# Four graph layers on one core: the message bias copied into PSUM by ScalarE, and 1/rms spread over the partitions by two DMAs

## What is computed

```python
# layer 0
agg = eps * x + adj @ x
h = silu(rmsnorm(agg @ W1 + b1) * rms_weight)      # 512 hidden columns
x = layernorm(x + h @ W2 + b2)
# layer 1
x_conv = relu(bn(conv17(relu(bn(conv1(x))))) + x)
s = x @ w_se.T + b_se
A = exp(-squared_distances(s))
msg = relu(x @ w_msg.T + b_msg)
x = layernorm(x + gru([x_conv, A @ msg], x))
# layer 2: three hops with adj / row_sum(adj), weighted sum, leaky relu
# layer 3
x = layernorm(x + relu(((1 + eps) * x + adj @ x) @ W1 + b1) @ W2 + b2)
```

## Time and profile before

| what | us |
|---|---|
| median of 3 runs (lowest, highest) | 1133.11 (1129.41, 1134.9) |
| the profiled execution's own time | 1131.74 |
| its span in the trace | 1129.9 |

### The profile page before, as it was taken

How to read it: one execution, slowest core, us unless ns; L and a number is a source line. 1 busy time by engine, 2 the same in 40 slices (tenths; PEclk the granted TensorE clock), 3 DMA queues, 4 the chain that set the end, 5 groups by cost and what they waited for, 6 DMA issues and landing times.

```text
span 1129.9 us, 24862 instructions
## 1 busy us (share of the span) xinstructions
PE 1074.6 (95%) x8043; PEld 961.1 (85%) x8043; DVE 818.6 (72%) x2549; ACT 709.2 (63%) x1305; POOL 613.6 (54%) x652
## 2 busy tenths in 40 slices
PE   7899999999999959989999999999999999999875
PEld 6799999999999959967888888888888888888764
DVE  4477787777778733624788787878787878788984
ACT  4445555555555532345677787877777777777765
POOL 1244433434343306634466777777777777777865
PEclk9999999999999989989999999999999999999999
DMA  4112323222322126841211121212121212100001
GB/s 162 57 48 84 94 94 95 84 90 90 95 94 85 57 82 205 249 153 48 60 45 57 48 67 48 66 48 67 48 66 48 67 48 67 48 20 19 20 29 38
DMA packets 64190, 84.45 MB, mean 75 GB/s; under 512 B 6464, under 2 KB 33472, under 8 KB 63808
## 3 DMA queue, kind: packets, MB, share of 16 engines
q1 hardware_dynamic: 64064, 82.86, 23.2%
HBM read 57.14 MB, written 25.69 MB: 73 GB/s over the span
## 4 chain that ended last, share of the span: by engine, by line
PE 89%; DVE 4%; issue 3%; POOL 2%; ACT 1%; DMA 1%; SPq 0%; ACTq 0%; DVEq 0%; POOLq 0%
PE banks L160 18%; PE banks L154 12%; PE banks L155 10%; PE banks L156 10%; PE banks L515 10%; PE banks L774 4%; PE banks L684 3%; PE banks L543 3%; PE banks L608 3%; PE banks L659 2%; PE banks L485 2%; PE banks L637 2%; PE banks L575 1%; PE banks L611 1%; PE banks L613 1%
## 5 line engine op out<-in xcount | busy, mean ns | idle before, releaser
L167 POOL TENSOR_TENSOR rstd<-ve,minus_half 128x4 f32<-128x4 f32 x128 | 131.1, 1025 | 52.5 <-DVE ve L1088 49.1
L167 POOL TENSOR_TENSOR r_rms<-ms,minus_half 128x4 f32<-128x4 f32 x32 | 32.3, 1009 | 223.9 <-DVE ms L1052 223.9
L515 PE MATMUL banks<-w,s 128*128 128x128 f32 x768 | 101.2, 275 | 0.4 <-DVE y L1066 0.4
L515 PEld LDWEIGHTS banks<-w,s 128*128 128x128 f32 x768 | 95.6, 192 | 3.3 <-issue 0.5
L154 PE MATMUL banks<-agg_hi,w_hi 128*128 128x512 f32 x192 | 84.3, 439 | 3.2 <-ACT agg_hi L164 3.0
L1078 DVE BATCH_NORM_STATS2 stats<-y 128x6 f32<-128x128 f32 x384 | 82.6, 276 | 2.2 <-POOL y L1445 2.0
L156 PE MATMUL banks<-agg_hi,w_lo 128*128 128x512 f32 x192 | 76.1, 396 | 0.0
L155 PE MATMUL banks<-agg_lo,w_hi 128*128 128x512 f32 x192 | 76.1, 396 | 0.0
L1420 POOL TENSOR_TENSOR y<-ya,yb 128x512 f32<-128x512 f32 x32 | 41.6, 1299 | 63.2 <-PE banks L724 62.5
L1406 POOL TENSOR_TENSOR x_lo<-x1c,x_hi 128x512 fp32r<-128x512 f32 x32 | 41.2, 1287 | 62.7 <-ACT x_hi L164 62.7
L160 PE MATMUL banks<-at,x_rows 128*128 128x128 f32 x512 | 69.7, 280 | 3.9 <-DVE agg_lo L1040 3.0
(11 more groups left out here) (197 smaller groups left out, 3369.8 us busy)
## 6 DMA issues: line engine op xcount, KB each, us to landing
at<-in_at SPq DMA_DIRECT2D x32, 256.0 KB, 2.9
x_rows<-in_x SPq DMA_DIRECT2D x32, 256.0 KB, 2.9
x_scratch<-x SPq DMA_DIRECT2D x32, 256.0 KB, 3.2
ad<-in_ad SPq DMA_DIRECT2D x32, 256.0 KB, 2.6
x1c<-x_scratch SPq DMA_DIRECT2D x32, 256.0 KB, 2.6
atc<-in_at SPq DMA_DIRECT2D x32, 256.0 KB, 3.0
yh<-yh_scratch SPq DMA_DIRECT2D x64, 128.0 KB, 3.4
out<-out_rows SPq DMA_DIRECT2D x32, 256.0 KB, 2.0
```

What stands on the lines that cost most here:

```text
L167: return nc.gpsimd.tensor_tensor(to[:], base[:], minus_half[:], ALU.pow)
L515: last = pe.matmul(bank[7][:, g, :], s[c][:, g, :], w2[:, c, :], start=(c == 0 and g == 0), stop=(c == H0 - 1), skip_group_check=True)
```

## The change

1. PE's and ACT's `spread_rms` go. SP stores r_rms (128 x 4, one value of 4 bytes each) to DRAM as 4 x 128, waits for it, and loads these 2 KB into each of 128 partitions of rv, which becomes a ring of two. `rms` on POOL waits for the store of the group before.
2. `messages` has no bias product. ACT's `message_bias` copies the bias row, repeated for the four graphs, into bank 4, and the products add to it. One product at the start of the third stage marks the bank as written.
3. All engines' orders in the first and third stage are new, and the banks are dealt out anew, with the waits of `free` that belong to them. Depths in turns change: `hidden` 2 and 3, `down`, `residual0`, `apply0`, `row_sums` come a turn later in the first stage, `gram` in the turn of its group; agg_hi and agg_lo are double. x_rows has five tiles, ad has one.
4. The start flag in `by_graph` stands on the first of four products. The three startup tiles share memory with hn. POOL's `minus_mean` counts on r2's and r3's semaphores. The preparation of `msg_bias` and `pick` (two memsets, two copies on ACT, one subtraction on DVE) goes.

Tiles and constants:

```diff
-        X_RING, AT_RING, AD_RING, X1_RING = 4, 2, 2, 2
+        X_RING, AT_RING, AD_RING, X1_RING, RV_RING = 5, 2, 1, 2, 2
...
             for g in range(G):
-                last = pe.matmul(psum[:, g, :], lhs(g), rhs(g), start=True, stop=True)
+                last = pe.matmul(psum[:, g, :], lhs(g), rhs(g), start=(g == 0), stop=(g == G - 1),
+                                 skip_group_check=True)
...
+        agg = rows("agg")
+        agg_hi, agg_lo = ([rows(f"agg_{n}{i}", F32R) for i in range(2)] for n in ("hi", "lo"))
+        rv = [rows(f"rv{i}") for i in range(RV_RING)]
...
-        TURNS1 = GROUPS + 11
+        TURNS1 = GROUPS + 12
```

SP:

```diff
             def load_ad(k):
                 until(sp, "row_sum", k - AD_RING)
                 sp.dma_start(ad[k % AD_RING][:], w["ad"][k]).then_inc(ad_in[k % AD_RING], 16)
+            def store_rms(k):
+                until(sp, "r_rms", k)
+                landed(sp, rv_in, k - 2)
+                sp.dma_start(rms_dram[k].rearrange("g n -> n g"), r_rms[:],
+                             allow_slow_non_contiguous=True).then_inc(rms_stored[k % 2], 16)
+            def load_rv(k):
+                landed(sp, rms_stored, k)
+                until(sp, "hn2", k - RV_RING)
+                sp.dma_start(rv[k % RV_RING][:], rms_dram[k].unsqueeze(0).to_broadcast([P, G, P])
+                             ).then_inc(rv_in[k % RV_RING], 16)
...
                 stage(load_at, t + 2)
                 if t >= 2:
                     stage(load_x, t + 1)
+                stage(store_rms, t - 1)
+                stage(load_rv, t - 1)
+                stage(load_ad, t + 1 - 12)
                 stage(store_x1, t - 6)
-                stage(load_ad, t + 2 - 11)
```

PE, first stage:

```diff
-            def spread_rms(k):
-                until(pe, "r_rms", k)
-                free(pe, ("hcp", k - 7), ("rv", k - 1))
-                for g in range(G):
-                    last = pe.transpose(bank[4][:, g, :], r_rms[:, g:g + 1].to_broadcast([P, P]), ident[:])
-                last.then_inc(sem["spread"], 1)
...
             def conv1(k):
                 until(pe, "x1", k)
-                free(pe, ("rv", k + 6), ("hcp", k - 1))
-                by_graph(pe, bank[4], lambda g: x1[k % X1_RING][:, g, :], lambda g: conv1_w[:]
+                free(pe, ("ms", k + 7), ("prod", k + 7), ("hcp", k - 1))
+                by_graph(pe, bank[5], lambda g: x1[k % X1_RING][:, g, :], lambda g: conv1_w[:]
...
                 if half == 0:
-                    free(pe, ("hn3", k + 8), ("xh0", k - 1))
+                    free(pe, ("hn0", k + 8), ("xh0", k - 1))
                 else:
-                    free(pe, ("hn2", k + 8), ("ms", k + 8), ("xh1", k - 1))
-                psum = flat(bank[(3, 1)[half]])
+                    free(pe, ("hn1", k + 8), ("xh1", k - 1))
...
             for t in range(TURNS1):
                 stage(neighbours, t)
+                stage(down, t - 4, 3)
+                stage(hidden, t - 2, 3)
+                stage(square_sums, t - 1)
+                stage(hidden, t - 2, 2)
                 stage(conv1, t - 8)
+                stage(transform, t - 10, 1)
+                stage(down, t - 3, 0)
+                stage(hidden, t - 1, 1)
+                stage(transform, t - 10, 0)
+                stage(down, t - 3, 1)
+                stage(x1_t, t - 5)
+                stage(hidden, t - 1, 0)
                 stage(down, t - 3, 2)
-                stage(gram, t - 1)
-                stage(x1_t, t - 5)
-                stage(down, t - 3, 3)
-                stage(transform, t - 10, 0)
-                stage(transform, t - 10, 1)
-                stage(hidden, t - 1, 0)
-                stage(hidden, t - 1, 3)
-                stage(square_sums, t - 1)
-                stage(hidden, t - 1, 1)
-                stage(hidden, t - 1, 2)
-                stage(down, t - 2, 0)
-                stage(spread_rms, t - 1)
-                stage(down, t - 2, 1)
+                stage(gram, t)
```

PE, third stage (of the order only the lines of the new one):

```diff
             def messages(k):
                 landed(pe, x1c_in, k)
-                free(pe, ("z0", k - 8), ("c2_res", k), ("v", k - 2), ("msg", k - 1))
-                pe.matmul(flat(bank[7]), pick[:], flat(msg_bias), start=True, stop=False, skip_group_check=True)
+                until(pe, "msg_set", k)
                 for g in range(G):
-                    last = pe.matmul(bank[7][:, g, :], x1c[k % X1C_RING][:, g, :], msg_w[:], start=False,
+                    last = pe.matmul(bank[4][:, g, :], x1c[k % X1C_RING][:, g, :], msg_w[:], start=False,
                                      stop=(g == G - 1), skip_group_check=True)
                 last.then_inc(sem["msg_ps"], 1)
...
+            landed(pe, x1c_in, 0)
+            pe.matmul(flat(bank[4]), ident[:], flat(x1c[0]), start=True, stop=True).then_inc(set_pe, 1)
...
                 stage(codes, t)
+                stage(inverse, t - 1)
+                stage(hidden3, t - 9, 1)
+                stage(gate_x, t - 2, R_GATE)
+                stage(messages, t - 1)
                 stage(down3, t - 9, 0)
+                stage(distances, t)
                 stage(y1_t, t - 5)
                 stage(down3, t - 9, 1)
+                stage(gate_nmp, t - 2, R_GATE)
+                stage(hop2, t - 6)
+                stage(hidden_n, t - 2)
+                stage(gate_conv, t - 2, R_GATE)
+                stage(gather3, t - 8)
+                stage(prop_in, t - 5)
+                stage(hop3, t - 6)
                 stage(gate_nmp, t - 2, N_GATE)
                 stage(gate_x, t - 2, Z_GATE)
                 stage(gate_conv, t - 2, N_GATE)
                 stage(gate_nmp, t - 2, Z_GATE)
+                stage(hop1, t - 5)
                 stage(gather, t - 1)
+                stage(hidden3, t - 8, 0)
                 stage(gate_conv, t - 2, Z_GATE)
```

ACT (of the orders only the new ones):

```diff
-            def spread_rms(k):
-                until(act, "spread", k)
-                until(act, "hn2", k - 1)
-                copy(rv[:], bank[4][:]).then_inc(sem["rv"], 1)
...
+                stage(silu, t - 3, 2)
+                stage(silu, t - 3, 3)
                 stage(full, t)
                 stage(high, t)
+                stage(x1_full, t - 6)
+                stage(spectrum_of, t - 10, 1)
+                stage(conv1, t - 9)
+                stage(spectrum_of, t - 10, 0)
+                stage(silu, t - 2, 1)
+                stage(silu, t - 2, 0)
...
+            def message_bias(k):
+                free(act, ("ghn", k - 2), ("msg", k - 1))
+                if k == 0:
+                    act.wait_ge(set_pe, PE_PROP + 1)
+                copy(bank[4][:], msg_row.unsqueeze(1).to_broadcast([P, G, P])).then_inc(sem["msg_set"], 1)
...
+                stage(factors, t, 0)
                 stage(factors, t, 1)
+                stage(hidden3, t - 9, 0)
+                stage(conv_high, t - 2)
+                stage(gate_z, t - 3)
+                stage(x1_high, t - 1)
                 stage(hidden3, t - 9, 1)
                 stage(message, t - 1)
+                stage(apply3, t - 10)
+                stage(edges, t)
+                stage(hidden_n, t - 2)
                 stage(gate_r, t - 2)
+                stage(agg3, t - 8)
+                stage(message_bias, t)
+                stage(apply2, t - 7)
                 stage(gate_n, t - 3)
+                stage(multiple, t - 5, 3)
+                stage(leaky_relu, t - 6)
                 stage(conv_full, t - 1)
+                stage(multiple, t - 5, 2)
+                stage(multiple, t - 5, 1)
+                stage(multiple, t - 5, 0)
                 stage(nmp_high, t - 1)
```

DVE, first stage:

```diff
-                until(dve, "rv", k)
+                landed(dve, rv_in, k)
                 until(dve, ("s0", "s1", "s2", "s3")[c], k - 1)
-                V.scalar_tensor_tensor(out=hn[c][:], in0=bank[(5, 0, 1, 3)[c]][:], scalar=column("b1", c), in1=rv[:],
+                V.scalar_tensor_tensor(out=hn[c][:], in0=bank[(3, 0, 2, 6)[c]][:], scalar=column("b1", c),
+                                       in1=rv[k % RV_RING][:],
                                        op0=ALU.add, op1=ALU.mult).then_inc(sem[("hn0", "hn1", "hn2", "hn3")[c]], 1)
...
             for t in range(TURNS1):
+                stage(apply0, t - 5)
                 stage(product, t - 1)
-                stage(apply0, t - 4)
-                stage(residual0, t - 3)
+                stage(normalise, t - 3, 2)
+                stage(residual0, t - 4)
                 stage(mean_square, t - 1)
-                stage(stats0, t - 3)
+                stage(normalise, t - 2, 1)
+                stage(stats0, t - 4)
+                stage(low, t)
+                stage(normalise, t - 2, 0)
+                stage(moments, t - 4, 0, LN_EPS)
+                stage(normalise, t - 2, 3)
+                stage(row_sums, t - 12)
                 stage(conv1_bias, t - 8)
-                stage(low, t)
-                stage(moments, t - 3, 0, LN_EPS)
-                stage(row_sums, t - 11)
-                stage(normalise, t - 1, 1)
```

(35 more changed lines are left out.)

235 lines of the change are left out of this document (94 added, 141 removed).

## The result

The changed kernel takes **1214.26 us** (median of four, 1211.53 to 1215.42) against 1132.44 us of the kernel before: ratio 1.0719, 95% interval 1.0694 to 1.0744. The forecast was 1115 (1101 to 1128). The profiled execution took 1214.68 us, its span is 1212.9 us.

A forecast was written before the change was run, and what follows sets the result against it. PE, busy 95% of the span, was taken to bound the full turns of the first and third stages. Terms -14.1 - 7.4 + 5 - 3 + 1 + 1 + 0.3 = -17.2 us took 1131.7 to 1114.5, called 1115 (1101 to 1128).

The forecast's parts named there:

- Transposes off PE: First stage: four transposes per group leave PE, 0.44 us each group in the chain, 32 x 0.44 = -14.1 us.
- Round trip: First stage: storing r_rms and loading rv takes 4 + 2.9 us, bounds 4.8 to 10.8, hidden behind other work: 0 us.
- Fill: Start of the first stage: normalise waits some 3 us, but PE's early turns are shorter: 0 (-2 to +3).
- Order and drain: First stage's drain: apply0 heads DVE's turn, so three turns get shorter, less some slow start: -3 us (-6 to 0).
- tight copies: First stage, full turns: spectrum copies out of banks 0 and 3 must be over in 1.3 us: +1 (0 to 3).
- Ring of ad: Start of second stage: one ad tile delays row sums and POOL's sixth negation, so PE waits: +5 us (0 to +8).
- Bias: Third stage: one 128x512 bias product per group leaves PE, 0.23 us in the chain, 32 x 0.23 = -7.4 us.
- Sum: Whole kernel: all terms together make -17.2 us, taking the profiled 1131.7 us to 1114.5.
- Rival A: First stage: 1/rms returns late, normalise waits each turn, low and gram behind it; slower, 1154 us at 13 us; chance 0.10.
- Rival B: First or third stage: tight handovers slip 0.3 to 0.5 us per turn, some 12 us: 1127 us; chance 0.14.
- C: Start of second stage: the single ad tile costs nothing: 1110 us, or 1105 with a faster drain; chance 0.12.
- D: First and third stages: waits replace each removed piece, PE's turns stay 11.56 and 18.94 us: 1133 us; chance 0.02.

The follow-up runs named there:

- apart: Changed kernel with the 4-byte pieces of r_rms stored 64 bytes apart and rv loaded from one fixed 2 KB row: 1115.08 us, ratio 0.9843.
- pe_spread2: Changed kernel with 1/rms spread again by four transposes on TensorE, ScalarE's copy of rv placed ahead of its relu: 1129.72 us, ratio 0.9973.
- bias_pe: store16 plus ScalarE reordering rv, the last five turns' ad loaded into freed x_rows tiles, and the message bias back on TensorE: 1124.68 us, ratio 0.9935.
- delay2: store16 with rv loaded three times, each load waited for before the next: 1210.53 us, ratio 1.0698.
- store16: Changed kernel with r_rms stored as 128 pieces of 16 bytes and rv read at a stride of four: 1124.89 us, ratio 0.9946.
- micro3: No computation, single stores timed alone: 4-byte pieces side by side or at steps, and 8-byte pairs; step of 8 bytes 3.0 us, of 64 bytes 1.8.

## Why the prediction was wrong

By its own steps, against apart, which differs from the changed kernel in the spacing of the stored pieces and in the row that is loaded:

- *Transposes off PE, -14.1:* pe_spread2 less apart is 1129.72 - 1115.08 = 14.6 us; turn 11.63 against 11.20 (forecast 11.13). Right.
- *Round trip, 4 + 2.9 = 7 us, covered, 0:* **this step failed.** Measured 9.9 + 5.1 = 15.0 us, outside the bounds of 4.8 and 10.8. The store is 5.9 us over its 4, the load 2.2 over its 2.9. I priced the pieces by the mean of all packets, 65 ns, though only 6464 of the 64190 packets before were under 512 bytes. For pieces that lie apart that gives too much (they land in 1.9 us), for neighbours 5.9 us too little, because their time doesn't lie in packets at all. No row of before had such a store, and I had written that down; but I made the upper end from the slowest transfer of another shape and then trusted it. The load was mis-sized mostly by the burst. It cost 99 us: 1214.26 - 1115.08.
- *Fill, 0:* right with a short trip (in apart mean_square stands 3.3 us behind its turn's start and that of turn 11 at 129.4, so turn 11 begins at 126.1 us; 125.2 forecast). With the long one it is the dearest part, since turns there are shorter and cover less. mean_square of group 10 stands at 168.4 us against 129.4 in apart (39 us lost), that of group 30 at 445.3 against 353.8 (52 more in 20 turns), and the second stage begins 101 us later (9 in the drain).
- *Order and drain, -3, and tight copies, +1:* in apart the first stage ends at 406.56 us, 17.6 before 424.16; the steps say 16.1. Right.
- *Ring of ad, +5:* the second stage is 69.2 us against 61.1, so 8, the upper end; PE's wait is 4.75 as forecast, undoing it gives back 6.6. Right in kind, low by 1.6 to 3.
- *Bias, -7.4:* bias_pe says 8.2; the third stage as a whole (with the +1 for its order and the 0.3 for the extra product) is 7.9 shorter, 6.1 forecast. Right in kind, low by 1 to 2.
- *Sum:* -17.2 from a span of 1129.9 gives 1112.7 us; apart's span is 1112.5. So without the trip the sum was right within 0.2 us; its terms were off by up to 3 us, and that they cancel is luck.

Rival A was what happened, and I gave it 0.10. It named the dear writes and the wait of normalise, but put low and gram behind that wait, where the chain has the transform that waits for hn1's bank, and its geometry was wrong. I had a loop of one turn and a cover of 11.7 us; the chain shows a loop over two turns, so a late microsecond is shared by two, while the fill, which I had left out, and the lower clock add. The cover (what the trip may take before PE waits for it), read from apart's chain, is 10.6 us (the sums end at 208.06, r_rms 1.36 later, and hn1 must begin 0.9 before the transform at 220.96). The price comes out the same in both pairs: changed kernel over apart 99.2 / (15.0 - 10.6) = 22.5 us per us, delay2 over store16 85.6 / (14.5 - 10.6) = 22. Both pairs lie about 4 us beyond the cover, so nothing here says that the price is the same at 1 us. My 30 us beyond 11.7 gives 1214 for 15.0, right only by luck, because cover and price were off in opposite ways. Rival B stayed out, C had no part (the ring costs), D had none.

## What to carry to other kernels

When a change sends a tiny array through memory to turn it, look at what lies next to what at the destination, not only at bytes and pieces: turn it on an engine first or keep the contiguous order, and store rows. A transfer of a form that no row shows gets a wide upper end, and if a loop through it decides, the rival deserves more than one in ten. Work out such a loop over as many turns as it spans, and for the fill, where the turns that should cover it are short.

## What was not expected of the hardware

- 4-byte writes side by side in memory: 512 take 7.9 to 10.2 us, 128 take 6.9; with a step of 8 bytes 3.0, of 64 bytes 1.8; reading them back in that form 2.1. In micro3 the DMA engines are through with the pieces 1.3 us after issue, side by side or 64 bytes apart, and show no packet until landing.
- A queue blocked in a wait makes its own traffic slow: loads of 256 KB need 2.7 us when they are spread (apart), 4.6 to 5.1 when SP releases them in a burst without any 4-byte piece (delay2), and 5.6 with the slow store beside them (the changed kernel).
- Reading rv at a stride of four floats takes VectorE from 744 to 1128 ns, ScalarE from 597 (a copy of the same size from a bank, in the changed kernel) to 1104. The Trainium skill ("SBUF — State Buffer", Door 1: The DMA port swizzle) gives SBUF lines of 16 bytes and a penalty for each access that goes to a new line, and at a stride of four floats every access does; the trace agrees, in that both reads are slower.
- Behind some waits PE's granted clock was 0.50, and the next product down took 1.71 instead of 0.89 us, about 1.8 us lost per such wait in the chain of the changed kernel; behind others of about the same length (1.7 to 2.3 us) it stayed at 0.89.
